# Attention and feed-forward kernel: x of FFN group 2 ahead of group 0's down product, V of the last CROSS2 group ahead of the turn, the last FFN group added and stored by tiles

## The chip, the core and the metric

The kernel runs on one core of a Trainium2 chip. The engines are TensorE (PE; PEld is its weight load), VectorE (DVE), ScalarE (ACT), GpSimd (POOL) and SyncE (SP, which here only issues DMAs). Each runs its own list of instructions in order; semaphores hold them together. The metric is the device time of one execution, in microseconds (us), as a median of several runs.

## What is computed

Two blocks follow each other on x (32 x 64 rows of 128) with a context (32 x 64 rows of 96). The first has self-attention, cross-attention with 16 heads of 64, and a GEGLU feed-forward part, each behind a layer norm. The second has a cross-attention with 16 heads of 8 and a feed-forward part with two residuals.

```python
def _L0_xattn_ref(x, context, Wq1, ..., b3):
    ...
    x = _attn(_ln(x, g1, b1), _ln(x, g1, b1), Wq1, Wk1, Wv1, Wo1, bo1) + x
    x = _attn(_ln(x, g2, b2), context, Wq2, Wk2, Wv2, Wo2, bo2) + x
    x = _geglu_ff(_ln(x, g3, b3), Wp, bp, Wf, bf) + x
    return x

def _L1_xattn_ref(x, xf, Wq, bq, ..., W2, b2):
    ...
    out = out @ Wo + bo
    h = (out - mu) * jax.lax.rsqrt(var + LN_EPS) * ln_g + ln_b
    h = jax.nn.gelu(h @ W1 + b1, approximate=False)
    ffn = h @ W2 + b2
    out = out + ffn
    return x + out
```

## The kernel before

The 2048 rows are 16 tiles of 128 rows, in 8 groups of 2 tiles. The five phases SELF, CROSS, GEGLU, CROSS2 and FFN run one after the other over the 8 groups, and each phase's first steps are done under the last groups of the phase ahead. "FFN 2" below is group 2 of the phase FFN. The order of work on each engine is written out by hand, once per engine, in the function `group` and a few functions for single groups (`seventh_cross2_group`, `last_cross2_group`). The class `Counts` repeats the order of the uses of the three PSUM banks `stage`, which rotate: a use takes the bank of the use three before it and waits until that one is copied out.

Steps that matter here:

- `x_step` on TensorE (L701) transposes a group's normalised rows `xn`; for CROSS2 also its context (L694). ScalarE scales it into `xT` (L1118) and rounds it into `src_h` (L1099), and POOL makes the remainder `src_r` (L1699, `rest_step`). The up products (L683 to L685) are three matmuls, of the h and r parts.
- In GEGLU and FFN, ScalarE makes the gelu of an up product (L1157, L1160), and in GEGLU DVE multiplies (L1406). `down_step` (L944) is the product with the second weight, and DVE adds it to the residual rows (L1498).
- The normalisation of a group three ahead is `stats_step` on DVE (L1356 to L1365, ending in `veps`), `rstd_step` on POOL (L1672) and `norm_step` on DVE (L1380), which fills the one buffer `xn` and so waits until the group before has been transposed out of it. For CROSS2, whose input is not normalised, `norm_step` is a copy (L1374).
- `bias_step` on POOL adds the bias to the residual rows (L1688), and in FFN also the older rows (L1692).
- In CROSS2: q and k (L758, L759), `v_step` (L769) with DVE's copy (L1399), `mask_step` on POOL (L1747), the scores (L805), DVE's maximum (L1422) and shift (L1429), ScalarE's exp (L1165), `cross2_turn_step` (L849, transposes the probabilities), the output (L913), `at_step` (L924) and `wo_step` (L934).
- A group of FFN begins on TensorE with a wait until ScalarE has copied all its earlier uses, and for FFN 1 until DVE has too. Its up products wait for `src_r`.
- SP stores each group of 128 KB when DVE has added it.

Of the kernel before, what the change touches and what calls it, by code (L numbers as in the profile page):

```python
# [22 lines left out]
ALU = mybir.AluOpType  # L23
# [9 lines left out]
T = 2  # L33
# [62 lines left out]
class Counts:  # L96
# [63 lines left out]
    def group(self, p, g):  # L160
# [32 lines left out]
        elif p == CROSS2:  # L193
            for name in ("scores", "out0", "norm", "atted"):
                self.tick(name, (p, g))
            for t in range(T):
                self.softmax(p, g, t)
            if 0 < g < GROUPS - 1:
                for i in (2, 3):
                    self.use("pt", p, g - 1, i)  # L200
            if g < GROUPS - 2:
                self.qk(p, g + 1)
                self.use("v", p, g + 1)
                if g == 0:
                    self.use("down", GEGLU, GROUPS - 1)
                self.x(p, g + 2)
                for i in (0, 1):
                    self.use("pt", p, g, i)
                if g > 0:
                    self.use("at", p, g - 1)  # L210
                    self.use("wo", p, g - 1)
            elif g == GROUPS - 2:
                self.qk(p, g + 1)
                for i in (0, 1):
                    self.use("pt", p, g, i)
                self.use("v", p, g + 1)
                self.use("at", p, g - 1)
                for i in (2, 3):
                    self.use("pt", p, g, i)
                self.use("wo", p, g - 1)  # L220
                self.x(FFN, 0)
            else:
                for i in (0, 1):
                    self.use("pt", p, g, i)
                self.use("at", p, g - 1)
                self.use("wo", p, g - 1)
                for i in (2, 3):
                    self.use("pt", p, g, i)
                self.x(FFN, 1)
                self.p(FFN, 0, range(4))  # L230
                self.use("at", p, g)
                self.p(FFN, 1, (0, 1))
                self.use("wo", p, g)
                self.p(FFN, 1, (2,))
                self.use("down", FFN, 0)
                self.x(FFN, 2)
                self.p(FFN, 1, (3,))
        elif (p, g) == (GEGLU, GROUPS - 2):
            self.p(p, g + 1, (0, 1))
            self.x(CROSS2, 0)  # L240
            self.p(p, g + 1, (2, 3))
            self.qk(CROSS2, 0)
            self.x(CROSS2, 1)
            self.use("down", p, g)
            self.use("v", CROSS2, 0)
        elif (p, g) not in ((GEGLU, 0), (GEGLU, GROUPS - 1), (FFN, 0)):
            if one:
                self.p(one.phase, one.first, (0, 1))
            if two:
                self.x(two.phase, two.first)  # L250
            if one and one.phase == p:
                self.p(one.phase, one.first, (2, 3))
            self.use("down", p, g)
# [37 lines left out]
def attention_blocks(nc, w, out):  # L291
# [3 lines left out]
    with ctx:  # L295
# [144 lines left out]
        high_w = sem("high_w")  # L440
        rest_w = sem("rest_w")
        stored = sem("stored")

        scale = {SELF: DH ** -0.5, CROSS: DH ** -0.5, CROSS2: H1 ** -0.5}
        kdim = {SELF: D, CROSS: C}
# [101 lines left out]
        def _(sp):  # L547
# [68 lines left out]
                store(Step(FFN, 0, turn, GROUPS // 2 - 1))  # L616
                store(Step(FFN, 1, turn, GROUPS // 2 - 1))
            store(Step(FFN, GROUPS - 2))
            store(Step(FFN, GROUPS - 1))
            sp.wait_ge(stored, 16 * GROUPS)  # L620


        @block.tensor
        def _(pe):
# [313 lines left out]
            def down_step(s):  # L938

                bank = home("down", s)  # L940
                wd = wf if s.phase == GEGLU else w2
                for t in range(T):
                    for i in range(FF // 128):
                        last = nc.tensor.matmul(bank[:, t * D:(t + 1) * D],  # L944
                                                hid[s.parity][:, i, t * ROWS:(t + 1) * ROWS], wd[:, i, :],
# [22 lines left out]
            def seventh_cross2_group(s):  # L968
# [2 lines left out]
                cross2_turn_step(before, 1)  # L971
                qk_step(one, s)
                cross2_out_step(before, 1)
                cross2_turn_step(s, 0)
                v_step(one, s)
                cross2_scores_step(one, s)
                pe.wait_ge(atted, cnt.at("atted", before))
                cross2_out_step(s, 0)
# [5 lines left out]
            def last_cross2_group(s):  # L984
# [12 lines left out]
                at_step(s, s)  # L997
                p_step(second, s, (0, 1))
                wo_step(s, s)
                p_step(second, s, (2,))  # L1000
                pe.wait_ge(act, cnt.at("act", first, 3, kind="up"))
                down_step(first)
                x_step(third, s)
                p_step(second, s, (3,))

            def group(s):
# [90 lines left out]
        def _(sc):  # L1097
# [139 lines left out]
            def last_cross2_group(s):  # L1237
# [10 lines left out]
                x_high_step(second)  # L1248
                load_table(ACT.Gelu)
                p_step(first)  # L1250
                p_step(second, (0, 1, 2))
                x_step(third)
                p_step(second, (3,))

            def group(s):
                one, two = s.ahead(1), s.ahead(2)
# [87 lines left out]
        def _(ve):  # L1344
# [143 lines left out]

            def down_step(s):

                ve.wait_ge(full, cnt.at("full", s, kind="down"))
                if s.phase == GEGLU:
                    ve.wait_ge(biased, cnt.at("biased", s))
# [57 lines left out]
            def group(s):  # L1551
# [58 lines left out]
                else:  # L1610
# [4 lines left out]
                    if three:  # L1615
                        stats_step(three)
                    if s.phase == GEGLU:
                        p_step(one, (1, 2, 3))
                    if three:
                        norm_step(three, two)  # L1620
                    if s.is_group(GEGLU, GROUPS - 2):
                        norm_step(s.ahead(3), two)
                    down_step(s)
                    if s.is_group(GEGLU, GROUPS - 2):
                        p_step(two)
# [37 lines left out]
        def _(gp):  # L1663
# [96 lines left out]
            def group(s):  # L1760
# [8 lines left out]
                if s.is_group(CROSS2, GROUPS - 1):  # L1769
# [3 lines left out]
                    rest_step(two)  # L1773
                    norm_step(s.ahead(3), two)
                    bias_step(one)
                    bias_step(two)
                    return
                if s.is_group(CROSS, GROUPS - 1):
# [98 lines left out]
```

## Time and profile before

| | |
|---|---|
| median of 3 runs | 451.22 us (450.65 to 452.02) |
| profiled execution | 450.97 us, span 449.3 us |
| TensorE busy | 434.4 us (97%) |
| DVE, ACT, POOL busy | 352.9, 318.8, 201.8 us |
| granted TensorE clock | 1.00 |

The span runs from the first to the last instruction. TensorE is busy in nearly all of it, at the full clock, so the few places where it waits, and what comes ahead of its first and behind its last matmul, are what can be read as lost; work of the other engines counts only where TensorE waits for it. In a timeline row, a number in square brackets is the engine's idle time just ahead, with the engine that ended it. A row can hold several matmuls (x16). The products of 32-bit values take two recorded passes each, so the profile counts twice as many as the program's order does.

### The profile page before, as it was taken

The numbers are of one execution on the slowest core, as the hardware profiler recorded it, in microseconds if no ns is written. First come the engines' busy times: TensorE is split into PE (matmuls) and PEld (weight loads), VectorE is DVE, ScalarE is ACT, GpSimd is POOL, SyncE is SP. The second block draws the span as 40 slices with busy tenths as digits, with TensorE's granted clock in tenths as the row PEclk, the third lists the DMA queues.
The fourth block names the chain that finished last, engine by engine and source line by source line (L and its number), as shares of the span: only waits on it lengthen the run. The fifth ranks groups of instructions, "written<-read, shape, count | busy, mean of one in ns | idle before, by whom it ended". The sixth has DMA issues, their size and how long they took to land.

```text
span 449.3 us, 17107 instructions
## 1 busy us (share of the span) xinstructions
PE 434.4 (97%) x7513; PEld 399.4 (89%) x7513; DVE 352.9 (79%) x649; ACT 318.8 (71%) x587; POOL 201.8 (45%) x226
## 2 busy tenths in 40 slices
PE   8999999999999999999999999999999999999897
PEld 7979999898999999989989899889999777778797
DVE  4888889688797887978978789896784788898471
ACT  5686676777778768787677776876546576777763
POOL 1883332555345634555352533523342232152782
PEclk9999999999999999999999999999999999999999
DMA  7202021110200000000000000000000000000011
GB/s 230 58 4 85 3 85 28 53 48 4 63 4 4 10 3 11 12 3 10 12 2 12 3 10 13 3 3 1 2 1 19 10 12 19 4 1 4 13 36 47
DMA packets 14623, 10.61 MB, mean 24 GB/s; under 512 B 5188, under 2 KB 13592, under 8 KB 14552
## 3 DMA queue, kind: packets, MB, share of 16 engines
q1 hardware_dynamic: 14120, 9.48, 7.3%
q8 instruction: 58, 0.95, 0.9%
q10 hardware_dynamic: 432, 0.07, 0.1%
q14 instruction: 13, 0.11, 0.1%
HBM read 8.50 MB, written 1.05 MB: 21 GB/s over the span
## 4 chain that ended last, share of the span: by engine, by line
PE 88%; DVE 6%; ACT 2%; issue 2%; POOL 1%; DMA 1%; POOLq 0%
PE stage L683 12%; PE stage L684 11%; PE stage L685 11%; PE scp L865 8%; PE scp L788 7%; PE scp L837 6%; PE scp L944 6%; PE out0p L885 4%; PE out0p L913 4%; PE out0p L887 3%; PE out0p L886 3%; PE stage L849 3%; PE scp L805 2%; DVE pr L1417 1%; PE stage L934 1%
## 5 line engine op out<-in xcount | busy, mean ns | idle before, releaser
L1734 POOL TENSOR_TENSOR pr<-pr,rc 128x1024 f32<-128x1024 f32 (+1 forms) x32 | 59.1, 1867 | 76.5 <-DVE rc L1447 76.4
L1165 ACT ACTIVATE pr<-pr 128x1024 f32<-128x1024 f32 x48 | 50.8, 1059 | 36.7 <-DVE pr L1417 30.1
L1672 POOL TENSOR_TENSOR rstd<-veps,neghalf 128x2 f32<-128x2 f32 x32 | 22.8, 714 | 70.8 <-DVE veps L1365 70.6
L1099 ACT ACTIVATE vt<-stage 64x512 f32<-64x512 f32 x83 | 49.2, 592 | 4.8 <-PE stage L685 1.2
L1461 DVE COPY vt<-stage 64x512 f32<-64x512 f32 x45 | 31.2, 694 | 21.8 <-PE stage L685 20.9
L1412 DVE TENSOR_REDUCE mx<-scp 128x16 f32<-128x1024 f32 x32 | 39.2, 1224 | 8.9 <-PE scp L788 8.5
L1099 ACT ACTIVATE ot_h<-scp 128x512 fp32r<-128x512 f32 x64 | 33.4, 600 | 13.3 <-PE scp L865 13.3
L1467 DVE TENSOR_TENSOR ot_r<-scp,ot_h 128x512 fp32r<-128x512 f32 x64 | 40.0, 683 | 2.3 <-ACT ot_h L1099 1.0
L1099 ACT ACTIVATE k_of_heads<-stage 128x512 f32<-128x512 f32 x62 | 36.9, 598 | 5.4
L1417 DVE TENSOR_TENSOR pr<-scp,mx 128x1024 f32<-128x1024 f32 x32 | 39.2, 1224 | 1.1
L1445 DVE TENSOR_REDUCE sm<-pr 128x16 f32<-128x1024 f32 x32 | 38.0, 1188 | 0.0
L865 PEld LDWEIGHTS scp<-pt,vt 64*64 64x64 f32 x2048 | 32.2, 135 | 5.8 <-issue 5.5
L865 PE MATMUL scp<-pt,vt 64*64 64x64 f32 x2048 | 34.7, 220 | 2.6 <-issue 1.5
L788 PEld LDWEIGHTS scp<-k_of_heads,q_of_heads 64*64 64x64 f32 x2048 | 31.5, 135 | 6.2 <-issue 5.3
L788 PE MATMUL scp<-k_of_heads,q_of_heads 64*64 64x64 f32 x2048 | 33.9, 220 | 0.5 <-issue 0.5
L837 PE MATMUL scp<-ident,pr 128*128 128x128 f32 x256 | 33.7, 274 | 0.2 <-POOL pr L1734 0.2
L1747 POOL TENSOR_TENSOR masked_k<-kT,fourmask 128x1024 f32<-128x1024 f32 x8 | 15.2, 1894 | 40.4 <-ACT kT L1144 40.4
L1099 ACT ACTIVATE q_of_heads<-stage 128x512 f32<-128x512 f32 x49 | 27.2, 589 | 7.2 <-PE stage L685 7.1
L837 PEld LDWEIGHTS scp<-ident,pr 128*128 128x128 f32 x256 | 29.0, 140 | 3.2 <-POOL pr L1734 0.5
L1472 DVE COPY pt<-scp 128x512 f32<-128x512 f32 x32 | 22.1, 691 | 9.6 <-PE scp L837 9.6
L1688 POOL TENSOR_TENSOR rows<-rows,bias 128x256 f32<-128x256 f32 x32 | 23.4, 734 | 1.2
L1422 DVE TENSOR_REDUCE mx<-scp 128x16 f32<-128x1024 f32 x16 | 19.6, 1222 | 4.1 <-PE scp L805 3.9
(266 smaller groups left out, 1398.8 us busy)
## 6 DMA issues: line engine op xcount, KB each, us to landing
ctx_in<-in_ctx_dram SPq DMA_DIRECT2D x16, 96.0 KB, 2.0
masked_k<-in_L_xattn_Wo_dram SPq DMA_DIRECT2D x2, 512.0 KB, 3.8
out_dram<-rows SPq DMA_DIRECT2D x8, 128.0 KB, 1.8
rows<-in_x_dram SPq DMA_DIRECT2D x1, 768.0 KB, 9.4
pr<-in_L_xattn_Wq_dram SPq DMA_DIRECT2D x1, 512.0 KB, 4.9
pr<-in_L_xattn_Wk_dram SPq DMA_DIRECT2D x1, 512.0 KB, 6.2
pt<-in_L_xattn_Wv_dram SPq DMA_DIRECT2D x1, 512.0 KB, 7.6
rows<-in_L_xattn_Wq_dram SPq DMA_DIRECT2D x1, 512.0 KB, 5.1
```

The costliest lines, as they stand in the source:

```text
L683: nc.tensor.matmul(dst, wh, mh, start=start, stop=False)
L684: nc.tensor.matmul(dst, wh, mr, start=False, stop=False)
L685: return nc.tensor.matmul(dst, wr, mh, start=False, stop=True)
L788: last = nc.tensor.matmul(scp[64 * b:64 * b + 64, 2 * t + e, a * N:(a + 1) * N], heads_of[0][h, a, n], heads_of[1][h, a, n], start=True, s ...
L837: last = nc.tensor.transpose(scp[:, 2 * t + c, q * 128:(q + 1) * 128], pr[t][:, a * 128:(a + 1) * 128], ident[:, :])
L865: last = nc.tensor.matmul(banks[i][64 * e:64 * e + 64, m * ROWS + b * N:m * ROWS + (b + 1) * N], vt[h, 2 * t + b, (2 * m + e) * DH:(2 * m ...
L1099: return nc.scalar.activation(dst, s, ACT.Copy)
L1165: nc.scalar.activation(pr[t][:, :], pr[t][:, :], ACT.Exp, scale=scale[s.phase]).then_inc(exped, 1)
L1412: nc.vector.tensor_reduce(mx[:, t, :], sc3, AX.X, ALU.max).then_inc(maxed, 1)
L1417: nc.vector.tensor_tensor(halves(pr[t][:, :]), sc3, mx[:, t, :, None].to_broadcast([ROWS, H, N]), ALU.subtract).then_inc(shifted, 1)
L1467: nc.vector.tensor_tensor(ot_r[:, :, i, t, :], bank, of.bitcast(F32), ALU.subtract).then_inc(dve, 1)
L1734: nc.gpsimd.tensor_tensor(p, p, rc[:, t, h:, None].to_broadcast([ROWS, H - h, N]), ALU.mult)\
```

## The change

The change has four parts, three of order and one of tiles.

1. End of GEGLU: DVE copies the rows of CROSS2 1 into `xn` ahead of its products of GEGLU 7's hidden chunks 2 and 3, instead of behind them.
2. CROSS2 6: TensorE does `v_step` of CROSS2 7 ahead of `cross2_turn_step(s, 0)`. The rotation of the `stage` banks changes with it for three uses.
3. CROSS2 7: TensorE does `x_step` of FFN 2 ahead of the up product of chunk 2 of FFN 1 and of the down product of FFN 0, and ScalarE's two steps of x follow the gelu of chunk 1 of FFN 1 instead of chunk 2. POOL does `rest_step` of FFN 2 and `rstd_step` of FFN 3 ahead of `bias_step` of FFN 1, instead of behind it.
4. FFN 7: the two tiles of the down product go to two PSUM banks. DVE adds each tile when it is there, and SP stores each tile (64 KB) by itself.

```diff
@@ Counts.group (the bank order)
                 self.qk(p, g + 1)
+                self.use("v", p, g + 1)
                 for i in (0, 1):
                     self.use("pt", p, g, i)
-                self.use("v", p, g + 1)
...
                 self.use("wo", p, g)
+                self.x(FFN, 2)
                 self.p(FFN, 1, (2,))
                 self.use("down", FFN, 0)
-                self.x(FFN, 2)
                 self.p(FFN, 1, (3,))
@@ SP
-            store(Step(FFN, GROUPS - 1))
-            sp.wait_ge(stored, 16 * GROUPS)
+            last = Step(FFN, GROUPS - 1)
+            for t in range(T):
+                if t == 0:
+                    sp.wait_ge(first_added, 1)
+                else:
+                    sp.wait_ge(dve, cnt.at("dve", last, kind="down"))
+                sp.dma_start(o[:, last.at(T) + t, :],
+                             row_slice(rows2, last, 0, T)[:, t * D:(t + 1) * D]).then_inc(stored, 16)
+            sp.wait_ge(stored, 16 * (GROUPS + 1))
@@ TensorE, down_step, seventh_cross2_group, last_cross2_group
                 for t in range(T):
+                    if s.is_group(FFN, GROUPS - 1) and t == 1:
+                        last.then_inc(first_down, 1)
+                        bank = scp[:, 0, :]
                     for i in range(FF // 128):
...
                 cross2_out_step(before, 1)
+                v_step(one, s)
                 cross2_turn_step(s, 0)
-                v_step(one, s)
                 cross2_scores_step(one, s)
...
                 wo_step(s, s)
+                x_step(third, s)
                 p_step(second, s, (2,))
                 pe.wait_ge(act, cnt.at("act", first, 3, kind="up"))
                 down_step(first)
-                x_step(third, s)
                 p_step(second, s, (3,))
@@ ScalarE, last_cross2_group
-                p_step(second, (0, 1, 2))
+                p_step(second, (0, 1))
                 x_step(third)
-                p_step(second, (3,))
+                p_step(second, (2, 3))
@@ DVE, down_step and group
+                if s.is_group(FFN, GROUPS - 1):
+                    ve.wait_ge(summed2, cnt.at("summed2", s))
+                    ve.wait_ge(first_down, 1)
+                    r = row_slice(rows2, s, 0, T)
+                    nc.vector.tensor_tensor(r[:, 0:D], home("down", s)[:, 0:D], r[:, 0:D],
+                                            ALU.add).then_inc(first_added, 1)
+                    ve.wait_ge(full, cnt.at("full", s, kind="down"))
+                    nc.vector.tensor_tensor(r[:, D:GR], scp[:, 0, D:GR], r[:, D:GR], ALU.add).then_inc(dve, 1)
+                    return
...
                     if s.phase == GEGLU:
-                        p_step(one, (1, 2, 3))
+                        p_step(one, (1,))
+                    if s.is_group(GEGLU, GROUPS - 2):
+                        norm_step(s.ahead(3), two)
+                    if s.phase == GEGLU:
+                        p_step(one, (2, 3))
                     if three:
                         norm_step(three, two)
-                    if s.is_group(GEGLU, GROUPS - 2):
-                        norm_step(s.ahead(3), two)
@@ POOL, group
                     norm_step(s.ahead(3), two)
                     bias_step(one)
+                    return
+                if s.is_group(FFN, 0):
+                    rest_step(two)
+                    rstd_step(three)
+                    bias_step(one)
                     bias_step(two)
                     return
```

The order on TensorE in CROSS2 6, before. `vb` and `pt` are V and the turned probabilities, `cT1` is the context of CROSS2 7, `pr0` the probabilities of the first tile of CROSS2 6:

```order
L913 MATMUL out0p<-vb1,pt1 64x18 x16
L849 MATMUL stage1<-ident,pr0 128x128 x4
L849 MATMUL stage2<-ident,pr0 128x128 x4
L769 MATMUL stage0<-wv1_by_parity,cT1 64x64 x8
L805 MATMUL scp<-masked_k,qT1 64x256 x16
```

and now:

```order
L922 MATMUL out0p<-vb1,pt1 64x18 x16
L778 MATMUL stage1<-wv1_by_parity,cT1 64x64 x8
L858 MATMUL stage2<-ident,pr0 128x128 x4
L858 MATMUL stage0<-ident,pr0 128x128 x4
L814 MATMUL scp<-masked_k,qT1 64x256 x16
```

V of CROSS2 7 (`wv1_by_parity`) stands ahead of the eight transposes of `pr0`, and their banks are others.

The order on TensorE around the last steps of CROSS2 7, before. `src1` is FFN 1, `xn` here FFN 2, and `hid0` the hidden values of FFN 0:

```order
L934 MATMUL stage2<-wo1,attT 128x128 x2
L683 MATMUL stage1<-src1h,w1_h 128x256
L684 MATMUL stage1<-src1r,w1_h 128x256
L685 MATMUL stage1<-src1h,w1_r 128x256
L944 MATMUL scp<-w2,hid0 128x128 x8
L701 MATMUL scp<-ident,xn 128x128 x2
L683 MATMUL stage2<-src1h,w1_h 128x256
L684 MATMUL stage2<-src1r,w1_h 128x256
L685 MATMUL stage2<-src1h,w1_r 128x256
```

and now:

```order
L943 MATMUL stage2<-wo1,attT 128x128 x2
L710 MATMUL scp<-ident,xn 128x128 x2
L692 MATMUL stage1<-src1h,w1_h 128x256
L693 MATMUL stage1<-src1r,w1_h 128x256
L694 MATMUL stage1<-src1h,w1_r 128x256
L956 MATMUL scp<-w2,hid0 128x128 x8
L692 MATMUL stage2<-src1h,w1_h 128x256
L693 MATMUL stage2<-src1r,w1_h 128x256
L694 MATMUL stage2<-src1h,w1_r 128x256
```

The transposes of `xn` stand ahead of the up product of chunk 2 and of the down product.

The order on POOL from the norm of FFN 2 to the rstd of FFN 4, before. The pair L1688 and L1692 is one `bias_step`, and the pairs are those of FFN 0, 1 and 2 in that order:

```order
L1714 TENSOR_TENSOR xn<-xn,rstd0 128x256
L1688 TENSOR_TENSOR rows2<-rows2,bias 128x256
L1692 TENSOR_TENSOR rows2<-rows2,rows 128x256
L1688 TENSOR_TENSOR rows2<-rows2,bias 128x256
L1692 TENSOR_TENSOR rows2<-rows2,rows 128x256
L1672 TENSOR_TENSOR rstd1<-veps1,neghalf 128x2
L1699 TENSOR_TENSOR src0r<-xT0,src0h 128x256
L1688 TENSOR_TENSOR rows2<-rows2,bias 128x256
L1692 TENSOR_TENSOR rows2<-rows2,rows 128x256
L1672 TENSOR_TENSOR rstd0<-veps0,neghalf 128x2
```

and now (lines 1695, 1711, 1715 and 1722 are 1672, 1688, 1692 and 1699 of before):

```order
L1737 TENSOR_TENSOR xn<-xn,rstd0 128x256
L1711 TENSOR_TENSOR rows2<-rows2,bias 128x256
L1715 TENSOR_TENSOR rows2<-rows2,rows 128x256
L1722 TENSOR_TENSOR src0r<-xT0,src0h 128x256
L1695 TENSOR_TENSOR rstd1<-veps1,neghalf 128x2
L1711 TENSOR_TENSOR rows2<-rows2,bias 128x256
L1715 TENSOR_TENSOR rows2<-rows2,rows 128x256
L1711 TENSOR_TENSOR rows2<-rows2,bias 128x256
L1715 TENSOR_TENSOR rows2<-rows2,rows 128x256
L1695 TENSOR_TENSOR rstd0<-veps0,neghalf 128x2
```

The remainder of FFN 2 (`src0r`) and the rstd of FFN 3 (`rstd1`) stand ahead of the second pair, and the second and third pair follow each other.

## Rows read from the trace of the kernel before

**Rows 1.** Busy by stretch, 427 to 441 us; per engine busy (count), clock, DMA share, GB/s.
```profile
427.00:441.00 14.00, 14.00 (x124) 13.99 (x124) 8.56 (x29) 9.97 (x25) 10.92 (x17) 1.00 0.13 38
```

**Rows 2.** TensorE's waits, 339 to 449.3 us: total, times, longest.
```profile
PE out0p L683 <- POOL src0r L1699: 1.6, 1, 1.6
PE stage L849 <- ACT pr L1165: 0.9, 1, 0.9
PE out0p L913 <- ACT pt L1099: 0.4, 1, 0.4
PE scp L694 <- DVE xn L1374: 0.4, 1, 0.4
```

**Rows 3.** Timeline, end of GEGLU: start, length, engine, line, operation, count [idle before].
```profile
345.64 0.28 DVE L1374 COPY xn<-rows 128x256 f32<-128x256 f32 x1
...
345.98 0.42 PE L694 MATMUL scp<-ident,ctx_in 128*96 128x128 f32 x2 [0.42 <-DVE xn L1374]
...
346.52 1.89 POOL L1747 TENSOR_TENSOR masked_k<-kT,fourmask 128x1024 f32<-128x1024 f32 x1 [5.65 <-ACT kT L1144]
...
348.44 0.42 DVE L1498 TENSOR_TENSOR rows<-scp,rows 128x256 f32<-128x256 f32 x1 [2.52 <-PE scp L944]
...
348.97 1.12 PE L805 MATMUL scp<-masked_k,qT 32*64 32x256 f32 x32
```

**Rows 4.** Timeline, CROSS2 6, TensorE and DVE.
```profile
403.72 1.23 DVE L1429 TENSOR_TENSOR pr<-scp,mx 128x1024 f32<-128x1024 f32 x1
...
403.85 1.06 PE L849 MATMUL stage<-ident,pr 128*128 128x128 f32 x8 [0.92 <-ACT pr L1165]
...
404.84 0.69 PE L769 MATMUL stage<-wv_by_parity,cT 96*64 96x64 f32 x16
...
405.46 1.12 PE L805 MATMUL scp<-masked_k,qT 32*64 32x256 f32 x32
```

**Rows 5.** Timeline, end of CROSS2 and start of FFN.
```profile
419.49 0.36 PE L683 MATMUL stage<-src1h,w_h 128*128 128x256 f32 x1
...
421.71 0.38 PE L701 MATMUL scp<-ident,xn 128*128 128x128 f32 x2
...
422.17 0.28 PE L685 MATMUL stage<-src1h,w_r 128*128 128x256 f32 x1
422.29 0.60 DVE L1380 TENSOR_SCALAR xn<-rows,mv,rstd 128x128 f32<-128x128 f32 x2
...
423.05 0.46 ACT L1160 ACTIVATE hid<-stage,cols 128x256 f32<-128x256 f32 x1
423.22 0.72 POOL L1699 TENSOR_TENSOR src0r<-xT,src0h 128x256 fp32r<-128x256 f32 x1 [1.05 <-ACT src0h L1099]
...
424.09 0.36 PE L683 MATMUL out0p<-src0h,w_h 128*128 128x256 f32 x1 [1.65 <-POOL src0r L1699]
...
425.41 0.70 POOL L1672 TENSOR_TENSOR rstd<-veps,neghalf 128x2 f32<-128x2 f32 x1
```

**Rows 6.** Timeline, FFN: DVE's norms and adds, TensorE's x of FFN 7.
```profile
426.22 1.14 DVE L1380 TENSOR_SCALAR xn<-rows,mv,rstd 128x128 f32<-128x128 f32 x2 [2.25 <-POOL rstd L1672]
...
427.80 0.42 DVE L1498 TENSOR_TENSOR rows<-scp,rows 128x256 f32<-128x256 f32 x1 [0.44 <-PE scp L944]
...
430.05 1.45 DVE L1380 TENSOR_SCALAR xn<-rows,mv,rstd 128x128 f32<-128x128 f32 x2 [0.89 <-POOL rstd L1672]
...
437.17 1.37 DVE L1380 TENSOR_SCALAR xn<-rows,mv,rstd 128x128 f32<-128x128 f32 x2 [0.89 <-POOL rstd L1672]
...
438.63 0.41 PE L701 MATMUL scp<-ident,xn 128*128 128x128 f32 x2
```

**Rows 7.** Timeline, DVE's last add.
```profile
446.57 0.42 DVE L1498 TENSOR_TENSOR rows<-scp,rows 128x256 f32<-128x256 f32 x1 [1.36 <-PE scp L944]
```

**Rows 8.** DMA issues: KB each, median us to landing.
```profile
out_dram<-rows SPq DMA_DIRECT2D x8, 128.0 KB, 1.8
```

**Rows 9.** DMA share in tenths, 447.9 to 448.7 us, 40 slices of 0.02 us.
```profile
DMA  0235769999999999999999875542110000000000
```

More of the change, by code:

```diff
@@ L442, in attention_blocks @@
         stored = sem("stored")
+        first_down = sem("first_down")
+        first_added = sem("first_added")
         scale = {SELF: DH ** -0.5, CROSS: DH ** -0.5, CROSS2: H1 ** -0.5}
```

## Prediction

> **What bounds the kernel now.** In the text, FFN 2 is group 2 of the phase FFN, x its transposition, up(1,3) the up product of FFN 1 for hidden chunk 3, down(1) its down product, norm(4) the normalisation of FFN 4, rest(2) POOL's rounding remainder src_r of FFN 2, bias(1) POOL's pair of adds (bias, then the first residual) for FFN 1, hid(1,3) ScalarE's gelu of up(1,3). I read first the busy time by stretch: from 427 to 441 us TensorE is busy for all 14.00 us at full granted clock [rows 1]. So time is won only where TensorE stands idle, or behind its last matmul. The waits of TensorE after 339 us are four, 0.4 + 0.9 + 0.4 + 1.6 us [rows 2]. Of these the change goes at three: the xn of CROSS2 1 (0.4), the exp of CROSS2 6 (0.9), and the src_r of FFN 2 (1.6). Its fourth part goes at what follows the last matmul. For each I read the timeline round the wait, and asked what is late next.
>
> **Part 1, the xn of CROSS2 1 a step earlier on DVE (end of GEGLU).** TensorE idles 0.42 us until 345.98, since DVE makes this copy at 345.64, behind its two last GEGLU products [rows 3]. It now makes it two products sooner, and the TensorE wait (0.42, at most some 0.15 more for the hand-over) goes. The copy costs DVE 0.28 in a stretch where DVE waits 2.52 before its next add, so it costs nothing. Next late are the first CROSS2 scores, at 348.97 [rows 3]. They need three things: TensorE's own order (348.97 less 0.42 to 0.57), DVE's add of GEGLU 6 (348.44 + 0.42 = 348.86, itself behind TensorE's down, so it moves with it to about 348.4), and POOL's mask, 346.52 + 1.89 = 348.41, which hangs on kT of CROSS2 0 and does not move [rows 3]. A hand-over to TensorE takes 0.06 (DVE's copy ends at 345.92, TensorE starts at 345.98) to 0.15 (POOL's src0r ends at 423.94, TensorE starts at 424.09) [rows 3, 5]. So the scores start at 348.41 + 0.15 = 348.56: **0.41 us** sooner. The bounds are 0.35 (a slow hand-over) and 0.50 (a fast one). All of CROSS2 then hangs on these scores and on its own steps, so I carry the 0.41 through it.
>
> **Part 2, V of CROSS2 7 ahead of the turn of CROSS2 6.** TensorE waits 0.92 us until 403.85 for exp; then it turns, does V (404.84) and the scores of CROSS2 7 (405.46) [rows 4]. V takes 405.46 - 404.84 = 0.62, and fits into the 0.92. Its bank in the new ring was held by a turn of CROSS2 5, which ScalarE copied before that wait; its DVE copy comes no sooner, since DVE has its order. The scores could then start at 404.84, but they wait for DVE's shift, 403.72 + 1.23 = 404.95 [rows 4], and a hand-over: about 405.08, **0.38 us** sooner. Lower bound 0.23, if DVE's own queue behind (V copy, then the next max), which gains less, sets the pace; upper 0.46, with a hand-over of 0.06. Behind that, the turns of CROSS2 7, the at and wo steps and the FFN's first products each wait for a step that itself hangs on TensorE, so all move by the same.
>
> **Part 3, x of FFN 2 earlier, and bias(1) behind rest(2) on POOL.** TensorE now does x(2) at 419.49, where it started up(1,2), and not at 421.71; POOL's rest(2) came 423.22 - 421.71 = 1.51 after that x, so it comes at 421.00 [rows 5]. The matmuls in between are the same, so up(1,3) still ends at 422.17 + 0.28 = 422.45. At the start of the next group TensorE waits for rest(2) and for hid(1,3). The first is now done at 421.7. The second was at 423.05, behind the two x steps on ScalarE; it now follows up(1,3) at about 422.5 and takes 0.46 [rows 5]. With the hand-over TensorE goes on at 423.1 in place of 424.09: **0.99 us there**.
>
> Most of that is given back, and this is where I chose. Count POOL: before, from rest(2) at 423.22 to rstd(4) at 425.41 are 2.19 us, rest and one bias pair; the rest takes 0.69 of it, the pair 1.50. Now rstd(3) (0.70) and bias(1) (1.50) stand there too: 421.00 + 2.19 + 0.70 + 1.50 = 425.39 [rows 5]. So rstd(4) comes no sooner than before. Rest(3), right behind it on POOL, now ends at about 426.8, and TensorE waits for it. More lasting is the chain on DVE: norm(4) starts at 426.22 behind rstd(4), then comes the add of down(1), then stats(5), then POOL's rstd(5), then norm(5). Before, the add of down(1) at 427.80 had waited 0.44 for TensorE [rows 6]; that slack goes. But norm(4) took 1.14 while POOL was idle at its start; with POOL busy norm(5) took 1.45 [rows 6], and rest(3) now starts with norm(4). So the add comes at about 427.5 and the chain gains 0.3. From norm(5) at 430.05 to norm(7) at 437.17 the chain takes 3.56 a group, and norm(7), some 1.4 long, ends just before x(7) at 438.63 [rows 6]: the chain is as late as TensorE there, so TensorE can keep only what the chain gains. I take **0.35 us** (0.15 to 0.45; the ends of the unknown are -0.1, no gain on DVE, and 0.99).
>
> Norm(3) moves under bias(1). It took 0.60 with POOL idle [rows 5], and may take the 1.45 of norm(5); it then ends at about 423.9, when TensorE comes to x(3). That cost is nothing so long as rest(3) is what TensorE waits for.
> The Trainium skill (SBUF — State Buffer, "Who interferes with whom") has such a DVE instruction and a POOL one exclude each other for a whole instruction, which agrees with 0.60 against 1.45. By that rule, with both POOL adds in front of norm(3), x(3) would be at about 424.6 and this part worth 0.15, the total 449.9.
>
> **Part 4, the last group by tiles.** The last add starts at 446.57, takes 0.42, and a store of 128 KB lands 1.8 after its issue [rows 7, 8]. Tile 0 is now added and stored under tile 1's matmuls, in another PSUM bank. What is left at the end is an add of 128 columns and a store of 64 KB. The add saves between 0 and 0.27; half of the columns, so I take 0.13. Of the store's time the packets move for some 0.6 (30 slices of 0.02 us with packets in them) [rows 9]; half the packets save up to 0.3. I take 0.25. The first store goes out while tile 1's matmuls still run, and is out of the way. Sum **0.38 us**, bounds 0.0 and 0.5, and below nothing by 0.1 if the second issue must wait for the first.
> The Trainium skill (DMA: Bandwidth & Descriptors, "Rules for kernel authors") speaks against this: transfers under 64 KB are mostly overhead, and are better joined. Its section "Anatomy of one DMA" has 2.0 us fixed and 436 KB in a us beyond, by which 64 KB less would save 0.15 and part 4 be worth 0.28; the trace lands 128 KB in 1.8, less than that fixed part alone, so I hold to the packets.
>
> **The sum.** 0.41 + 0.38 + 0.35 + 0.38 = 1.52 us. The profiled execution took 450.97 (span 449.3), 0.25 below the median of 451.22; it becomes 449.45, the median **449.7**. No DMA, instruction or matmul is added beyond one add and one store; code and waits elsewhere are the same.
>
> **The rivals.**
> - *The FFN gain is swallowed whole.* For: rstd(4) stays at 425.4, and the chain's slope against TensorE. Against: the 0.44 of slack at 427.80. Part 3 is 0: 450.05. Chance 0.17.
> - *The tail saves only the add.* The landing is mostly fixed. Against: the 0.6 of packets. Part 4 is 0.13: 449.95. Chance 0.11.
> - *TensorE keeps the full 0.99*, if norms under POOL's load are shorter than I count: 449.06. Chance 0.06.
> - *The head starts are lost in CROSS2*, DVE's and POOL's steps there setting the pace and not TensorE's. Against: only 0.4 of TensorE waits in 52 us. Only 0.73 is left of the 1.52: 450.49. Chance 0.04.
> - *Slower: x(2) comes early on TensorE, but its ScalarE step doesn't*, held behind the gelus of FFN 1. Then rest(2) stays at 423.22, and POOL has rstd(3) and two bias pairs after it: rstd(4) at 427.6, 2.2 late, the add of down(1) at about 429.8, 2.0 late, and x(7) with it. 451.22 - 1.17 + 2.0 = 452.05. It decides against the change once rest(2) starts after about 422.5. Against: in ScalarE's order only hid(1,0) and hid(1,1) stand ahead. Chance 0.04.
>
> **How the numbers follow.** Forecast 0.58, within it 449.3 to 450.4. The range of 449.0 to 450.7 takes in the forecast and all rivals but the slower one and the far edges of the others. A change of 0.3% (1.35 us, to 449.87) is about what a measurement of this kernel can tell from none. The forecast lies only 0.17 beyond that line, so of its 0.58 I give 0.42 to faster; 0.06 is the full FFN gain, 0.06 a part of the first two rivals. Faster 0.54, same 0.42, slower 0.04.
>
> **What would show it.** Part 1: no wait for xn at the end of GEGLU, scores of CROSS2 0 right behind POOL's mask. Part 2: V inside the exp wait, and the wait cut to about 0.3; scores of CROSS2 7 behind DVE's shift. Part 3: rstd(4) about 4.4 us after rest(2) starts; TensorE waits of some tenths for rest(3), and again near x(7); the stretch from 424 to the last down no shorter than before. Part 4: last add near 0.29, last landing about 1.55 after its issue. Wrong would be: rest(2) late, a new wait of more than 0.3 in CROSS2, or a second store landing after 1.8.

## The result, and the profile after

| | before | after |
|---|---|---|
| median, 6 runs each | 450.89 us (450.65 to 452.02) | 448.78 us (447.74 to 449.54) |
| ratio | | 0.9947, 95% interval 0.9929 to 0.9965 |
| profiled execution | 450.97 us, span 449.3 | 447.74 us, span 446.0 |

The change makes the kernel faster by 0.5%, where 0.3% was forecast, and the median lies 0.22 us below the range. The page after, its span and busy time:

```profile
span 446.0 us, 17109 instructions
...
PE 433.8 (97%) x7513; PEld 398.7 (89%) x7513; DVE 353.9 (79%) x650; ACT 318.4 (71%) x587; POOL 201.5 (45%) x226
```

The two profiles differ by 3.3 us, and the prediction's sum was 1.5. To see where they part, both traces are cut at one step: the start of POOL's first masked keys of CROSS2, 346.52 in [rows 3]. The only edit ahead of it moves one DVE copy, for which this step doesn't wait: it starts 1.55 us behind TensorE's product for kT in both (344.97 before, 343.23 after). What lies ahead is called the front, the rest of the span the back. The front is 346.52 before and 344.78 after: 1.74 us less with no edit in it that could make it so. The back is 449.3 - 346.52 = 102.78 before and 446.0 - 344.78 = 101.22 after: 1.56 less. (Spans are given to 0.1 us, so a back is good to 0.05.) The profiled execution of after (447.74) is the fastest of its six runs and that of before (450.97) lies near its median, so the 3.3 us overstate the change.

The back goes nearly as forecast. TensorE's waits from 336 us on (total, times, longest), against [rows 2]:

```profile
PE out0p L692 <- ACT hid L1172: 0.6, 1, 0.6
PE out0p L922 <- ACT pt L1111: 0.4, 1, 0.4
PE stage L858 <- ACT pr L1177: 0.4, 1, 0.4
PE scp L814 <- POOL masked_k L1770: 0.2, 1, 0.2
```

The wait for DVE's xn is gone, that for the exp fell from 0.9 to 0.4, and the 1.6 for the remainder of FFN 2 became 0.6 for hid(1,3). Timeline at the end of GEGLU, against [rows 3]:

```profile
342.04 0.28 DVE L1386 COPY xn<-rows 128x256 f32<-128x256 f32 x1
...
344.78 1.89 POOL L1770 TENSOR_TENSOR masked_k<-kT,fourmask 128x1024 f32<-128x1024 f32 x1 [5.65 <-ACT kT L1156]
...
346.82 1.12 PE L814 MATMUL scp<-masked_k,qT 32*64 32x256 f32 x32 [0.15 <-POOL masked_k L1770]
```

The scores start 346.82 - 344.78 = 2.04 behind the mask's start, before 348.97 - 346.52 = 2.45: 0.41 sooner, and what they wait for now is the mask. CROSS2 6, against [rows 4]:

```profile
400.62 0.67 PE L778 MATMUL stage<-wv_by_parity,cT 96*64 96x64 f32 x16
401.57 1.23 DVE L1441 TENSOR_TENSOR pr<-scp,mx 128x1024 f32<-128x1024 f32 x1
401.70 1.06 PE L858 MATMUL stage<-ident,pr 128*128 128x128 f32 x8 [0.42 <-ACT pr L1177]
...
402.85 1.12 PE L814 MATMUL scp<-masked_k,qT 32*64 32x256 f32 x32
```

V lies in the exp wait. The shift ends at 402.80 and the scores of CROSS2 7 start at 402.85, 58.07 behind the mask's start for 58.94 before: 0.87 sooner, 0.41 of part 1 and 0.46 of part 2. The start of FFN, against [rows 5]:

```profile
418.49 0.73 POOL L1722 TENSOR_TENSOR src0r<-xT,src0h 128x256 fp32r<-128x256 f32 x1 [1.19 <-ACT src0h L1111]
...
419.98 1.48 DVE L1392 TENSOR_SCALAR xn<-rows,mv,rstd 128x128 f32<-128x128 f32 x2
...
420.42 0.39 PE L692 MATMUL out0p<-src0h,w_h 128*128 128x256 f32 x1 [0.56 <-ACT hid L1172]
...
421.52 0.44 PE L710 MATMUL scp<-ident,xn 128*128 128x128 f32 x2
...
422.24 0.67 DVE L1377 TENSOR_SCALAR veps<-mv 128x2 f32<-128x2 f32 x1
...
422.51 1.95 PE L956 MATMUL scp<-w,hid 128*128 128x128 f32 x16
422.98 0.70 POOL L1695 TENSOR_TENSOR rstd<-veps,neghalf 128x2 f32<-128x2 f32 x1
423.65 0.72 POOL L1722 TENSOR_TENSOR src1r<-xT,src1h 128x256 fp32r<-128x256 f32 x1
...
424.43 0.38 PE L692 MATMUL out0p<-src1h,w_h 128*128 128x256 f32 x1
```

TensorE begins the up products of FFN 2 75.64 behind the mask's start, before 424.09 - 346.52 = 77.57: 1.93 sooner, of which 1.06 is part 3's (forecast 0.99). From there to the first up product of FFN 7 it takes 438.46 - 420.42 = 18.04, before 441.28 - 424.09 = 17.19. So **0.85 of the 1.06 is given back**, 0.21 kept. The tail, against [rows 7, 8] (the last row is a DMA issue: KB each, us to landing):

```profile
442.93 0.29 DVE L1507 TENSOR_TENSOR rows<-scp,rows 128x128 f32<-128x128 f32 x1 [0.54 <-PE scp L956]
443.75 0.29 DVE L1510 TENSOR_TENSOR rows<-scp,rows 128x128 f32<-128x128 f32 x1 [0.53 <-PE scp L956]
```
```profile
out_dram<-rows SPq DMA_DIRECT2D x2, 64.0 KB, 1.6
```

From the start of the last add to the end of the span are 446.0 - 443.75 = 2.25 us, before 449.3 - 446.57 = 2.73: 0.48 less. The four measured parts are 0.41 + 0.46 + 0.21 + 0.48 = 1.56, which is the back's whole difference.

### The profile page after: what moved, and what is told of

The parts are those of the page before. It is cut to its first block, busy times and chain, and to the rows that moved or that the text cites. A ratio compares the mean times of both kernels' runs of the same rounds, so it can differ in the third digit from the quotient of the medians.

```text
span 446.0 us, 17109 instructions
## 1 busy us (share of the span) xinstructions
PE 433.8 (97%) x7513; PEld 398.7 (89%) x7513; DVE 353.9 (79%) x650; ACT 318.4 (71%) x587; POOL 201.5 (45%) x226
## 4 chain that ended last, share of the span: by engine, by line
PE 84%; DVE 8%; issue 3%; ACT 2%; POOL 2%; DMA 1%; POOLq 0%; DVEq 0%
PE stage L692 12%; PE stage L694 11%; PE stage L693 11%; PE scp L874 7%; PE scp L797 7%; PE scp L846 6%; PE scp L956 5%; PE out0p L894 4%; PE out0p L922 3%; PE out0p L896 3%; PE out0p L895 3%; PE stage L858 2%; PE scp L814 2%; DVE pr L1429 1%; DVE mx L1424 1%
```

## The experiments

**Whose is the front?** Theory CHANCE: its 1.74 us differ from execution to execution. Rival BUILD: the edits behind it change the front of this build for good. The kernel before and the changed kernel were measured again, side by side and without any edit (12 runs each; the before that they are compared with has 35).

> The kernel before, unchanged, a second time. The span is cut at the start of POOL's first mask step of CROSS2 (346.52 us in the first profile of before, 344.78 in that of after), which none of the four edits touches: 'front' is what lies ahead, 'back' what lies behind (102.7 us before, 101.2 after). Theory CHANCE (the four edits give 1.57 us, all in the back, and the front varies from one execution to the next by TensorE's stalls marked 'issue'): ratio 1.000, back 102.7 within 0.1, front anywhere from 344.8 to 347, and not again 346.5 by rule. Theory BUILD (the front depends on how the program lies in memory, and is shorter in the changed build): front 346.5 within 0.2 again.

> The changed kernel, unchanged, a second time. CHANCE: back 101.2 within 0.1, front varies again, median 1.3 to 1.8 us below before (ratio 0.996 to 0.997). BUILD: front 344.8 within 0.3 again, and a ratio of 0.993 to 0.995.

The kernel before again: 450.68 us, ratio 0.9995 (0.9982 to 1.0007), front 346.09, back 102.81. The changed kernel again: 449.63 us (448.61 to 450.76), ratio 0.9969 (0.9960 to 0.9979), front 347.76, back 101.24. That is 1.11 us below the 450.74 of before, where CHANCE expected 1.3 to 1.8 (its ratio of 0.996 to 0.997 came true). The same changed kernel has the shortest and the longest front of all, 3 us apart, and its back agrees to 0.02. BUILD falls.

What differs in the front is seen in TensorE's timeline: stalls ended by nothing that the profile shows, marked issue. Before:

```profile
85.99 0.39 PE L865 MATMUL scp<-pt,vt 64*64 64x64 f32 x10 [0.65 <-issue]
...
109.51 0.32 PE L788 MATMUL scp<-k_of_heads,q_of_heads 64*64 64x64 f32 x2 [0.55 <-issue]
...
234.66 0.27 PE L865 MATMUL scp<-pt,vt 64*64 64x64 f32 x2 [0.88 <-issue]
...
316.81 0.36 PE L683 MATMUL stage<-src0h,wp_h 128*128 128x256 f32 x1 [0.91 <-issue]
```

The changed kernel, first profile:

```profile
108.10 0.33 PE L797 MATMUL scp<-k_of_heads,q_of_heads 64*64 64x64 f32 x2 [0.31 <-issue]
...
232.94 0.27 PE L874 MATMUL scp<-pt,vt 64*64 64x64 f32 x2 [0.62 <-issue]
...
315.08 0.36 PE L692 MATMUL stage<-src0h,wp_h 128*128 128x256 f32 x1 [0.91 <-issue]
```

The changed kernel, second profile:

```profile
86.55 0.34 PE L874 MATMUL scp<-pt,vt 64*64 64x64 f32 x8 [1.20 <-issue]
...
110.29 0.33 PE L797 MATMUL scp<-k_of_heads,q_of_heads 64*64 64x64 f32 x2 [0.79 <-issue]
...
235.70 0.27 PE L874 MATMUL scp<-pt,vt 64*64 64x64 f32 x2 [1.09 <-issue]
...
318.06 0.36 PE L692 MATMUL stage<-src0h,wp_h 128*128 128x256 f32 x1 [0.91 <-issue]
```

The places are the same (near 86 us the first profile of the changed kernel shows no stall), the lengths are not, but for the 0.91. The stalls that vary (those of 0.2 us and more, one of 0.24 to 0.28 near 259 us in some profiles among them) sum to 2.08, 0.93 and 3.32 us. In the 14 profiles of this study the front runs from 344.78 to 347.76; less its varying stalls it runs from 343.85 to 344.95. So they carry most of the front's spread.

The traces also show what goes ahead of each such stall. The profile's page counts the packets that carry instructions (16 KB each, in the whole span):

```profile
q8 instruction: 58, 0.95, 0.9%
```

Two stretches of 4 us each, in 40 slices of 0.1 us, ahead of the stall near 110 us: 105 to 109 us in the first profile of the changed kernel, and 107 to 111 us in that of `x_no_pool` (a run described below). The digit stands at the packet's start:

```profile
DMA  0000000500000000000000000000000000000000
q8 instruction: 1, 0.02, 1.4%
```
```profile
DMA  0000008000000000000000000000000000000000
q8 instruction: 1, 0.02, 2.1%
```

The first packet starts at 105.8 us and takes 0.9 (1.4% of 16 DMA engines' 4 us); the stall of 0.31 ends at 108.10. The second starts at 107.6 to 107.7 and takes some 1.35; the stall of 0.85 ends at 110.55. Each of the 42 varying stalls in the 14 profiles ends 2.3 to 3.0 us after the last such packet ahead of it has started, and 1.2 to 1.6 after that packet has ended. Near 86 us, 12 profiles have a stall and a packet that starts at 83.4 to 84.0; the two without a stall (the first of the changed kernel, and `pool_only` below) have theirs at 81.0 to 81.1 and at 85.4 to 85.5 instead. So the varying stalls look like TensorE waiting for its next instructions. No run changed how these arrive, so this is argued and not shown. The 0.91 is of another kind: no such packet starts in the 8.6 us ahead of its end.

**Do the parts add?** Theory ADDITIVE: each part is worth alone what it is worth in the sum. Rival ABSORBED: the last step hides what the order wins, or the other way. `order_only` is the change without part 4 (its diff is against the changed kernel), `tail_only` part 4 alone (its diff is against the kernel before):

```diff
@@ tail_only, TensorE (with DVE's and SP's part of the diff above)
+                    if s.is_group(FFN, GROUPS - 1) and t == 1:
+                        last.then_inc(first_down, 1)
+                        bank = scp[:, 0, :]
@@ order_only, SP (likewise TensorE and DVE)
             store(Step(FFN, GROUPS - 2))
-            last = Step(FFN, GROUPS - 1)
...
+            store(Step(FFN, GROUPS - 1))
+            sp.wait_ge(stored, 16 * GROUPS)
```

> Parts 1 to 3 of the change (the copy of xn, V, x of FFN 2 with the order on POOL), without part 4 (the last group by tiles). These add no instruction. By the profile of the changed kernel they gave 0.42 + 0.46 + 0.21 = 1.09 us. CHANCE: back 101.65 (102.74 less 1.09), ratio about 0.9976. BUILD: if it is part 4's added instructions and semaphores that shift the build, the front is 346.5 as before; if it is the order, 344.8.

> Part 4 alone: the last FFN group is added and stored by tiles. By the profile of the changed kernel it gave 0.48 us. CHANCE: back 102.26, ratio about 0.9989. BUILD with part 4 as its cause: front 344.8, ratio about 0.995.

Parts 1 to 3: 450.03 us, ratio 0.9983 (0.9971 to 0.9995), back 101.71. Part 4: 450.33 us, ratio 0.9990 (0.9977 to 1.0003), back 102.31. Against the 102.81 of before these are 1.10 and 0.50, together 1.60 for the 1.57 of both: they add, within what a back is good to. By the times alone part 4 can't be told from nothing; the back tells it.

**The single parts.** One profiled execution each of the kernel before with one of these edits:

```diff
@@ xn_only, DVE
-                        p_step(one, (1, 2, 3))
+                        p_step(one, (1,))
+                    if s.is_group(GEGLU, GROUPS - 2):
+                        norm_step(s.ahead(3), two)
+                    if s.phase == GEGLU:
+                        p_step(one, (2, 3))
                     if three:
                         norm_step(three, two)
-                    if s.is_group(GEGLU, GROUPS - 2):
-                        norm_step(s.ahead(3), two)
@@ v_only, TensorE (and the bank order)
+                v_step(one, s)
                 cross2_turn_step(s, 0)
-                v_step(one, s)
```

> Part 1 alone: DVE copies the rows of CROSS2 1 into xn two products sooner. 'Back' is the span behind the start of POOL's first mask step of CROSS2 (102.8 us in the two profiles of before; it repeats within 0.03). Theory ADDITIVE (each part gives its own gain at its own wait, and the next chain carries it to the end): back 102.38, 0.42 less. Rival ABSORBED (CROSS2 has slack of its own, and part 1 gives only with the others): back 102.6 or more.

> Part 2 alone: V of CROSS2 7 ahead of the turn of CROSS2 6. ADDITIVE: back 102.34, 0.46 less. ABSORBED: 102.6 or more.

Backs of 102.40 and 102.30: part 1 is 0.41 and part 2 is 0.51 of 102.81, within the rounding of the 0.41 and 0.46 that the changed kernel's trace gave. ABSORBED falls for both.

**Why does part 3 keep so little?** Theory CHAIN: the loop of DVE's norm, add and stats and POOL's rstd sets the pace, and POOL's new order delays it. Rival REST: what counts is when POOL's remainder (rest) is there for TensorE, and the new order brings rest(2) earlier. `x_pool` is part 3 alone, `x_no_pool` part 3 without this edit of POOL, which `pool_only` makes alone and which `no_pool_order` takes out of the changed kernel:

```diff
@@ POOL, group (at CROSS2 7 also without the bias_step(two))
+                if s.is_group(FFN, 0):
+                    rest_step(two)
+                    rstd_step(three)
+                    bias_step(one)
+                    bias_step(two)
+                    return
```

> Part 3 alone, with its order on POOL. ADDITIVE: back 102.59, 0.21 less: TensorE gains 1.06 at the first up product of FFN 2, and gives 0.85 back by x of FFN 7, since rstd(4) comes no sooner. ABSORBED: as without it, 102.8.

> Part 3 without its order on POOL: x of FFN 2 is early on TensorE and ScalarE, POOL keeps bias(1), rstd(3), rest(2), bias(2), rstd(4). Theory CHAIN (what counts is when rstd(4) starts, from which the DVE chain of norms, adds and statistics runs at 3.52 us a group): only one bias pair stands between rest(2) and rstd(4), so rstd(4) starts 0.3 to 0.7 sooner than in the changed kernel and the gain is 0.5 to 0.8 instead of 0.21: back 102.0 to 102.3. Rival REST (what counts is rest(2), which the order on POOL brings earlier): the first up product of FFN 2 comes later and the gain is smaller than 0.21, back 102.6 or more.

> The changed kernel with one edit taken back: POOL keeps the order of the kernel before round the start of FFN (bias(1), bias(2), rstd(3), rest(2), bias(3), rstd(4)). Counted from the start of POOL's first masked keys of CROSS2 to the end of the span, the changed kernel had 101.22 to 101.24 us in two profiles and the kernel before 102.78 to 102.81. Theory CHAIN+POOL (part 3's head start is worth about 1 us to the chain of DVE and POOL, and the new POOL order takes 0.75 of it back, since bias(1) and bias(2) stand ahead of rstd(4)): 100.5, within 0.25, and a time about 1.4 us below the changed kernel's neighbour in the same job less the chance of the front: ratio to before about 0.995. Theory NOISE (the 0.75 between the two kernels with part 3 alone was an accident of one profile): 101.2, ratio 0.997.

> The kernel before with POOL's new order at the start of FFN alone (rest(2), rstd(3), bias(1), bias(2)), while x(2) still comes behind down(0) on TensorE. Theory CHAIN+POOL: rstd(3) now stands behind rest(2), whose data come at about 423.2, so norm(3) starts some 2.3 us later and rstd(4) some 2 us later than before (427.5 for 425.41): 104.0 to 105.0 us behind the first masked keys, for 102.8 before. Theory ABSORBED (the chain has room at its start): 102.8 to 103.3.

The backs are 102.54, 101.78, 100.55 and 105.81. Part 3 alone is worth 0.27, and without POOL's new order 1.03, more than the 0.5 to 0.8 that CHAIN expected and the opposite of what REST expected. In the changed kernel that order costs 101.22 - 100.55 = 0.67, as expected (100.5), so NOISE falls. On the kernel before it alone costs 3.0, more than the 1.2 to 2.2 expected. There norm(3) waits for an rstd(3) behind rest(2), and TensorE waits 1.20 for the xn of FFN 3. What is beyond the expectation is the clock. The busy time of 425 to 429 us (its last three numbers are granted clock, DMA share and GB/s), and rows of TensorE:

```profile
425.00:429.00 4.00, 3.76 (x19) 3.76 (x20) 2.92 (x9) 1.72 (x4) 3.74 (x7) 0.57 0.01 4
```
```profile
425.24 0.47 PE L701 MATMUL scp<-ident,xn 128*128 128x128 f32 x2 [1.20 <-DVE xn L1380]
...
426.79 2.97 PE L944 MATMUL scp<-w,hid 128*128 128x128 f32 x16
...
427.38 0.72 POOL L1699 TENSOR_TENSOR src1r<-xT,src1h 128x256 fp32r<-128x256 f32 x1
...
429.52 0.36 PE L683 MATMUL out0p<-src1h,w_h 128*128 128x256 f32 x1
```

A mean of 0.57 over 4 us is some 3.4 us at 0.50, the lower of TensorE's two clocks (1.2 GHz), and the sixteen matmuls of L944 take 2.97 in place of 1.95. Ahead of it TensorE stood still twice, 1.64 us until 423.10 and 1.20 until 425.24; in the kernel before it stood still once, 1.65, and kept the full clock, as all other profiled runs do behind the cut as long as matmuls run. Rest(3) was there at 427.38 + 0.72 = 428.10, and TensorE began the next group only at 429.52. By these rows (an estimate) the low clock is worth 1.42 less a hand-over of 0.06, and the order by itself 3.0 - 1.36 = 1.6, within what was expected.

All four say that POOL's order hurts; part 3's gain is TensorE's alone. `no_pool_order` took 449.33 us, ratio 0.9959 (0.9944 to 0.9974). Where the changed kernel has norm(3) with 1.48, TensorE's x(3) 1.10 behind the first up product, and 4.01 to the next group, `no_pool_order` has:

```profile
421.97 1.19 DVE L1392 TENSOR_SCALAR xn<-rows,mv,rstd 128x128 f32<-128x128 f32 x2
...
422.53 0.37 PE L692 MATMUL out0p<-src0h,w_h 128*128 128x256 f32 x1 [0.58 <-ACT hid L1172]
...
423.34 0.38 PE L710 MATMUL scp<-ident,xn 128*128 128x128 f32 x2
...
424.18 0.70 POOL L1695 TENSOR_TENSOR rstd<-veps,neghalf 128x2 f32<-128x2 f32 x1 [0.29 <-DVE veps L1377]
...
425.97 0.36 PE L692 MATMUL out0p<-src1h,w_h 128*128 128x256 f32 x1
```

x(3) comes 0.81 behind the first up product, and the group takes 3.44. From these first up products (`out0p`, one a group) TensorE's time for each group from FFN 2 to FFN 6 is read off:

| kernel | groups 2 to 6, us | sum |
|---|---|---|
| before | 3.43, 3.43, 3.44, 3.42, 3.47 | 17.19 |
| after | 4.01, 3.52, 3.52, 3.52, 3.47 | 18.04 |
| no_pool_order | 3.44, 3.43, 3.44, 3.52, 3.46 | 17.29 |
| bias_behind | 3.78, 3.44, 3.42, 3.44, 3.48 | 17.56 |
| rstd_first | 5.01, 3.46, 3.43, 3.43, 3.43 | 18.76 |

TensorE's own pace is 3.43, that of the loop of DVE and POOL 3.52 (after, the norms start at 423.79, 427.30, 430.83 and 434.35). Before, the loop had 0.44 of room at its start [rows 6] and used it up by FFN 6. After, 0.58 is lost in the first group and 0.09 in each of the next three: 0.85. So both theories hold a part. The 0.27 is the loop's pace. In the first group TensorE loses 0.36 at the late x(3), behind norm(3), and then 0.22 more for rest(3), which ends at 423.65 + 0.72 = 424.37, just ahead of TensorE's 424.43. Rest(3) sets the whole 0.58: POOL works from 418.49 to 424.37 without a pause of more than 0.1 us (rest(2), rstd(3), bias(1), bias(2), rstd(4), rest(3)), so an earlier x(3) would only have made the wait behind it longer.

These short waits show in no list. TensorE's busy time by stretch, after, 424 to 438 us:

```profile
424.00:438.00 14.00, 14.00 (x121) 13.81 (x120) 9.18 (x30) 9.63 (x24) 10.80 (x16) 1.00 0.14 39
```

TensorE reads as busy for 14.00 of 14.00 us, as in [rows 1], though the loop holds it back by 0.09 a group. The matmuls' ends are modelled and lie past the next start (the first of FFN 2 is 0.39 long and the next starts 0.22 behind it), so a wait this short doesn't show.

**Can the loss be had back in another way?** Two more orders on POOL in the changed kernel:

```diff
@@ bias_behind: in FFN 0 without bias_step(two), and from FFN 1 on
                     if two:
                         rest_step(two)
+                    if s.phase == FFN and one:
+                        bias_step(one)
+                    elif two and s.phase != FFN:
                         bias_step(two)
@@ rstd_first: in FFN 0 without bias_step(two), and
+                if s.is_group(FFN, 1):
+                    rstd_step(three)
+                    bias_step(one)
+                    rest_step(two)
+                    bias_step(two)
+                    return
```

> The changed kernel, with POOL adding the bias of every FFN group one group later: FFN 0 ends with bias(1), and from FFN 1 on the order is rstd, rest, and the bias of the group before. So only one bias (1.5 us of POOL) stands between rstd(3) and rstd(4). Theory CHAIN+POOL: rstd(4) comes right behind veps(4), about 0.7 to 1.0 us earlier than in the changed kernel, and the end with it: 100.3 to 100.6 us behind the first masked keys, for 101.2; ratio to before about 0.995. Rival SHARED (POOL is busy beside DVE's norms all the same, so the gap is closed but every norm keeps its 1.36 to 1.48 us and something else comes last): 101.0 to 101.3, ratio 0.997.

> The changed kernel, with POOL's order in FFN 0 and 1 as rest(2), rstd(3), bias(1), rstd(4), bias(2), rest(3), bias(3); from FFN 2 on as in the changed kernel. Theory CHAIN+POOL: rstd(4) right behind veps(4), the gain in the chain 0.7 to 1.0 us, but rest(3) now comes 1.5 us later behind bias(2), which can take some of it from TensorE: 100.3 to 101.0 us behind the first masked keys. Rival SHARED: 101.0 to 101.3.

`bias_behind`: 449.19 us, ratio 0.9952 (0.9934 to 0.9971), back 100.79, which is 0.43 better than the changed kernel and short of the 0.6 to 0.9 expected. Its first group still takes 3.78, as norm(3) has its 1.48 and x(3) comes 1.10 behind the first up product: with rest(3) early, norm(3) by itself costs 3.78 - 3.43 = 0.35. The room behind it is back. `rstd_first`: 450.59 us, ratio 0.9988 (0.9976 to 0.9999), back 101.93, 0.7 worse than the changed kernel and outside both expectations. Its rstd(4) does come early (424.69, right behind veps(4)), but TensorE's first product of the next group reads:

```profile
427.63 0.39 PE L692 MATMUL out0p<-src1h,w_h 128*128 128x256 f32 x1 [0.96 <-POOL src1r L1722]
```

Rest(3) behind bias(2) is REST's wait in the open, 0.96 us. In the traces `no_pool_order` ends first behind the cut, 0.67 before the changed kernel. In the times it can't be told from it (ratios 0.9959, and 0.9947 and 0.9969 for the changed kernel, measured twice); both beat the kernel before.

## Why the prediction missed

**The time: the front.** The forecast of 449.7 took 1.52 off, and the back gave 1.56. The step that failed is the last one of the sum: it subtracts 1.52 from one profiled execution and from a median of three runs (451.22), takes all that lies ahead of 339 us as fixed, and sets the range by the terms of the sum alone. The measured 448.78 is 0.92 below the forecast. Of this 0.33 is the level (the six runs of before have 450.89, not 451.22), 0.04 is the back, and 0.55 is left, which no edit accounts for. TensorE's waits were read only from 339 us on. Read from 0 on, they held stalls of 0.65, 0.55 and 0.88 us marked issue, with no cause in the program's order, and the range needed their spread: fronts differ by 3 us for one and the same kernel, single runs of the kernel before range from 449.38 to 452.03 (35 runs), its medians are 450.89, 450.74 and 451.34, and the changed kernel's are 448.78 and 449.63. The second lies 0.07 from the forecast, but by luck in part: it is 1.11 below its own before, and not 1.52. The lower end of 449.0 left no room for the first. The direction was right, and two measurements clear of no change (0.9947 and 0.9969) say that 0.54 was a low chance for it; the second of these is just at the 0.3% line.

**Part 1** (0.41 forecast): 0.41. The wait for xn went, and the mask came last with a hand-over of 0.15.

**Part 2** (0.38): 0.46 in the changed kernel, its upper bound. The step that was off is the hand-over: DVE's shift ended at 402.80 and TensorE went on at 402.85, 0.05 later where 0.13 was counted.

**Part 3** (0.35 kept of 0.99): 0.21 kept of 1.06. To hold its times against the forecast's, add 1.74 + 0.41 + 0.46 = 2.61 to those of after. Rest(2) at 421.10 (forecast 421.00), the first up product at 423.03 (423.1), rstd(4) at 425.59 (425.39), add of down(1) at 427.68 (427.5): the steps are right, the first up product 0.07 early and the others 0.1 to 0.2 late. Rstd(4) is late because veps(4) took 0.67 while POOL added (0.17 with POOL idle), ending with POOL's add. The term that was mis-sized is the chain's gain, 0.3 forecast: it was 427.80 - 427.68 = 0.12 at the add of down(1) and 0.22 at the next one (431.42 before, 428.59 + 2.61 = 431.20 after), and that 0.22 is what TensorE kept. The slope was misread a little too: the 3.56 a group of before is one step of 3.60 and one of 3.52, and the loop's own pace is 3.52. The sentence that norm(3) under bias(1) costs nothing while rest(3) is what TensorE waits for holds, if only just: x(3) came 1.10 behind the first up product in place of 0.79, 0.31 late, and the wait for rest(3) came 0.22 behind that. `no_pool_order` shows what is to be had with neither: TensorE begins the up products 422.53 - 346.85 = 75.68 behind the mask's start, 1.02 sooner by part 3, and gives 0.10 back, so it keeps 0.92. The forecast saw that POOL's new order sets rstd(4) back, and left it at that; it did not ask what part 3 would be worth without it. The rival of the full 0.99 (chance 0.06) was what the change would have given without one of its own edits.
The Trainium skill (SBUF — State Buffer, "Who interferes with whom") has such DVE and POOL instructions exclude each other; norm(3) at 1.48 and veps(4) at 0.67 agree. The time that the prediction worked out by it (x(3) at 424.6, part 3 worth 0.15) was a little too dark: x(3) came at 424.13 and 0.21 was kept.

**Part 4** (0.38): 0.48, and 0.50 alone, near the upper bound. The add gave the 0.13 forecast, so the store gave 0.35 where 0.25 was taken (from 30 slices of [rows 9], which has 29). The landing itself fell from 1.8 to 1.6, which is some 0.2 of it; where the rest comes from is not shown. The first store did not hinder the second, as both landed in 1.5 to 1.6.
The Trainium skill (DMA: Bandwidth & Descriptors, "Anatomy of one DMA") gives its figures for DMAs that GpSimd issues, and these stores are issued by SP; the estimate of 0.28 by them was too low, as the trace shows 0.48.

**The rivals.** None came about. "Slower" needed rest(2) behind 422.5, and it came at 421.10. "Swallowed whole" was the nearest, 0.21 from what part 3 kept.

## What to carry to other kernels

Before a range is set, read the bounding engine's waits over the whole span, and take those marked issue as a term that changes from run to run. Compare traces from a common step just ahead of where the first edit can be felt: here such a back repeats to 0.03 us where times move by 1 us. Read the granted clock of the stretch before a loss is put down to an order: in `pool_only` about 1.4 of 3.0 us were the clock's. And when one edit hands a gain to an engine, price the order change that comes with it by itself: here 0.7 us of a 1.0 us gain went to a reorder on POOL that the gain did not need.

## What was not expected of the hardware

- TensorE's issue stalls stand at fixed places of the program. Those near 86 and 235 us last between nothing shown and 1.20 us, that near 110 between 0.26 and 0.87, while that near 317 took 0.91 in all 14 profiles. The varying ones end 1.2 to 1.6 us after a packet of the instruction queue has ended; that the packet is their cause was not tested.
- Two waits of TensorE close behind each other (1.64 and 1.20 us, with 0.9 us of matmuls between them) were followed by 3.4 us at half its clock in `pool_only`. One of 1.65 in the kernel before was not.
- A DVE instruction as small as 128x2 took 0.67 us in place of 0.17 while POOL was adding, so the tiny steps of such a loop are not free of POOL's load.
- TensorE can read 14.00 us busy of 14.00 and still be paced by another engine, 3.52 us a group for 3.43. The distance between like matmuls shows it; the busy time doesn't.
